# Six pieces of a recurrent scan's side work are put into other steps: the copy of the transposed tokens, a square, the modulation, two shift sums, the last block of x products and the head factors

## The reference

```python
def step(h, xt):                      # h: [8, 128]
    m = concatenate([xt, h], -1) @ weight + bias
    g = sigmoid(m[:, :128] + 1.0); c = tanh(m[:, 128:])
    h_new = g * h + (1.0 - g) * c
    return h_new, h_new
x = x + swapaxes(scan(step, cond, swapaxes(x, 0, 1))[1], 0, 1)
```

```python
ada = t_emb @ w_ada + b_ada           # six sections: sh, sc, g for attention; sh, sc, g for the MLP
xn = layer_norm(logmap0(x));  xm = expmap0(xn * (1 + sc_msa) + sh_msa)
q, k, v = (_to_heads(plin(xm, w, b)) for (w, b) in qkv)       # 16 heads of 8
attn = softmax(q @ k.T / sqrt(8));  out_h = expmap0(attn @ v)
x1 = mobius_add(x, expmap0(g_msa * logmap0(plin(_from_heads(out_h), w_o, b_o))))
xm = expmap0(layer_norm(logmap0(x1)) * (1 + sc_mlp) + sh_mlp)
out = mobius_add(x1, expmap0(g_mlp * logmap0(plin(plin(xm, w_f1, b_f1), w_f2, b_f2))))
x = x + out
```

## Time and profile before

| | us |
|---|---|
| three runs | 461.93, 460.52, 459.68 (median 460.52) |
| the profiled execution, from outside | 461.86 |
| its span | 460.0 |
| busy: DVE, PE, ACT, POOL | 342.5, 346.1, 275.7, 78.9 |
| first state of the scan, last state | 15.33, 294.03 |

### The profile page before, as it was taken

The page is one execution under the profiler, slowest core; times in us unless marked ns, Lnnn a source line. Parts: engine busy times, 40 slices in busy tenths (PEclk is TensorE's granted clock), DMA queues, the critical chain, the costliest instruction groups (busy, mean ns, idle before and its releaser), DMA issues.

```text
span 460.0 us, 11582 instructions
## 1 busy us (share of the span) xinstructions
PE 346.1 (75%) x3768; PEld 217.2 (47%) x3768; DVE 342.5 (74%) x1943; ACT 275.7 (60%) x1030; POOL 78.9 (17%) x152
## 2 busy tenths in 40 slices
PE   1887798797747786747897988989589889767932
PEld 1644565455535454535554645536344446446510
DVE  5578766786899887899887888744933388699883
ACT  2344654446557546557667566636688888954852
POOL 7000000021000021000022000032200115265580
PEclk9999999999999999999999999976679989996877
DMA  7201920010000000000000000000000000000102
GB/s 183 59 2 30 211 40 2 1 35 15 1 1 3 0 2 1 1 1 2 1 2 3 0 1 2 2 3 3 1 2 3 1 3 3 2 1 1 25 0 68
DMA packets 9118, 8.28 MB, mean 18 GB/s; under 512 B 1282, under 2 KB 7700, under 8 KB 9060
## 3 DMA queue, kind: packets, MB, share of 16 engines
q1 hardware_dynamic: 8964, 7.29, 6.9%
q0 software_dynamic: 96, 0.26, 0.2%
HBM read 6.47 MB, written 1.08 MB: 16 GB/s over the span
## 4 chain that ended last, share of the span: by engine, by line
DVE 45%; PE 31%; ACT 12%; issue 7%; POOL 2%; DMA 1%; SPq 0%; DVEq 0%; ACTq 0%; POOLq 0%
DVE guessed L1630 8%; DVE state L1630 8%; PE zb L847 5%; DVE sets L1651 5%; DVE rest L1649 5%; ACT sets L1323 4%; PE tb L974 3%; PE firsts L1145 3%; PE tb L785 3%; ACT prd L1487 2%; PE zb L1125 2%; PE zb L824 2%; PE firsts L1030 2%; ACT prd L1467 1%; PE tb L945 1%
## 5 line engine op out<-in xcount | busy, mean ns | idle before, releaser
L1323 ACT ACTIVATE sets<-zb 128x32 f32<-128x32 f32 x479 | 106.2, 227 | 110.5 <-PE zb L847 101.3
L847 PE MATMUL zb<-guessed,whh 128*128 128x8 f16 x960 | 64.7, 173 | 23.7 <-DVE guessed L1630 1.0
L1630 DVE TENSOR_TENSOR_SCAN state<-sets 128x32 f32<-128x32 f32 x256 | 57.0, 223 | 34.1 <-ACT sets L1323 32.5
L847 PE MATMUL zb<-rest,whh 128*128 128x8 f16 x480 | 51.8, 178 | 32.7 <-DVE rest L1649 31.6
L847 PEld LDWEIGHTS zb<-rest,whh 128*128 128x128 f16 x480 | 35.8, 113 | 80.1 <-DVE rest L1649 74.7
L1630 DVE TENSOR_TENSOR_SCAN guessed<-sets 128x32 f16<-128x32 f32 x255 | 57.4, 225 | 10.9 <-ACT sets L1323 2.9
L847 PEld LDWEIGHTS zb<-guessed,whh 128*128 128x128 f16 x960 | 44.5, 108 | 42.0 <-DVE guessed L1630 36.9
L1649 DVE TENSOR_TENSOR rest<-state,guessed 128x8 f16<-128x8 f32 x255 | 42.6, 167 | 8.7
L1487 ACT ACTIVATE prd<-zb 128x640 f32<-128x640 f32 x64 | 41.9, 711 | 5.7 <-PE zb L1125 5.0
L1651 DVE COPY sets<-state 128x32 f32<-128x32 f32 x255 | 45.0, 176 | 0.0
L641 POOL TENSOR_TENSOR stat<-mv 128x4 f32<-128x4 f32 x4 | 0.8, 202 | 219.5 <-DVE mv L1761 219.5
(11 more groups left out here) (370 smaller groups left out, 693.1 us busy)
## 6 DMA issues: line engine op xcount, KB each, us to landing
mod<-ada_rows SPq DMA_DIRECT2D x4, 768.0 KB, 11.0
resid<-in_x_dram SPq DMA_DIRECT2D x6, 128.0 KB, 3.6
ffz<-shift_rows SPq DMA_DIRECT2D x4, 131.0 KB, 3.2
out_dram<-state SPq DMA_DIRECT2D x8, 64.0 KB, 2.1
out_dram<-early SPq DMA_DIRECT2D x8, 64.0 KB, 2.1
yy<-in_L_cond_w_ada_dram SPq DMA_DIRECT2D x1, 384.0 KB
early<-in_L_cond_weight_dram SPq DMA_DIRECT2D x2, 128.0 KB
resid<-in_x_dram POOLq DMA_DIRECT2D x2, 128.0 KB, 3.5
```

The source lines that it names most:

```text
L847: return pe.matmul(bank[:, 256 * k + i:256 * k + i + NB], whh[:, half, k, :], h, start=False, stop=False, skip_group_check=True)
L1323: return act.activation(view(sets[:, n, 3:4], [39, 2], [38, 2], [4, NB]), view(bank[:, i:i + 1], [256, 2], [0, 2], [1, NB]), ACT.Tanh, sca ...
L1630: return dve.tensor_tensor_scan(dst, *scan_terms(n), 0.0, ALU.mult, ALU.add)
```

## The change

Six pieces are put elsewhere; none is added or taken away, and each computes what it did.

- `uevac` goes from 29 to 28: ACT copies the transposed tokens a tick earlier, in the slot that had the square of tile 1. That square goes behind it, into the slot of tick 29.
- `modulate` goes from 23 to 22: DVE's four instructions each stand a tick earlier. What they wait for (`tok_xn`) isn't moved.
- PE gets a `yield` behind the last shift product, so that `x_part(2)` begins at tick 77 instead of 76, and all its twelve pieces stand a tick later.
- DVE's two shift sums go from tick 79, where both stood, to ticks 84 and 85.
- In the scan's chunks the first of the two head factor instructions goes into the half step ahead of the guess, the second stays.

```diff
--- before.py
+++ after.py
@@ -74,8 +74,8 @@
 
 
 TOK = dict(
-    transpose=1, resid=5, moments=7, norm=10, artanh=12, rho=19, xn=21, modulate=23, utrans=26,
-    uevac=29, usq=(25, 27), clip=29, qkv=(29, 30, 31, 32, 33, 34, 35, 36), yevac=(31, 33, 35,
+    transpose=1, resid=5, moments=7, norm=10, artanh=12, rho=19, xn=21, modulate=22, utrans=26,
+    uevac=28, usq=(25, 27), clip=29, qkv=(29, 30, 31, 32, 33, 34, 35, 36), yevac=(31, 33, 35,
     37), qsq=(32, 34, 36, 38), qreduce=(34, 36, 38, 40), factor=42, scale=(50, 51, 56, 57),
     high=(51, 52, 57, 59), low=(52, 54, 58, 60), stack=(54, 56, 60, 62), queries=(56, 60, 62,
     64), keys=(58, 61, 63, 65), values=(62, 63, 64, 65, 66, 67, 68, 68), xna=21,
@@ -924,6 +924,7 @@
                 yield
                 pe.matmul(ob[:, 0:NB], gw[:, 0:D], shT[:, :], start=True, stop=True)\
                     .then_inc(shift_ps, 1)
+                yield
                 for c in range(2, NC):
                     yield from at_ticks(now, CH * (c - 1) + 8)
                     yield from x_part(c)
@@ -1401,13 +1402,15 @@
                     yield from at_ticks(now, base + T["usq"][1])
                     act.wait_ge(tok_u, c + 1)
                     squares_of((0,))
-                    if c < NC - 1:
-                        yield
-                    squares_of((1,)).then_inc(tok_usq, 1)
+                    if c == NC - 1:
+                        squares_of((1,)).then_inc(tok_usq, 1)
                     yield from at_ticks(now, base + T["uevac"])
                     act.wait_ge(tok_uT_ps, c + 1)
                     act.activation(tuT[:, :, :], tb[:, 1, :].rearrange("p (j t) -> p j t", j=NJ),
                                    ACT.Copy).then_inc(tok_uT, 1)
+                    if c < NC - 1:
+                        yield
+                        squares_of((1,)).then_inc(tok_usq, 1)
                     for j in range(NJ):
                         n = NJ * c + j
                         yield from at_ticks(now, base + T["qsq"][j])
@@ -1676,11 +1679,12 @@
                     if q < 3:
                         yield from whole(now)
                 i.then_inc(ada_sb, 1)
-                yield from at_ticks(now, 79)
+                yield from at_ticks(now, 84)
                 dve.wait_ge(shift_sb, 1)
                 sh = ada[:, 3 * D:4 * D]
                 dve.tensor_tensor_reduce(shift_junk[:, 0, :], sh, sh, 1.0, 0.0, ALU.mult, ALU.add,
                                          shift[:, D:D + 1])
+                yield from whole(now)
                 dve.tensor_tensor_reduce(shift_junk[:, 1, :], sh, shG[:, :], 1.0, 0.0, ALU.mult, ALU.add,
                                          shift[:, D + 1:D + 2]).then_inc(shift_rows, 1)
                 yield
@@ -1900,10 +1904,16 @@
                     i = dve.scalar_tensor_tensor(r, t, 1.5, r, ALU.add, ALU.mult)
                 done_(i)
                 mark = done[0]
-                yield from at_ticks(now, base + T["hfac"])
+                yield from at_ticks(now, base + T["hfac"] - (0.5 if in_scan else 0))
                 settle(mark)
-                settled(dve.tensor_scalar(ht[:, NH4:NA4], hy[:, NH4:NA4], C_HEAD * M_CLIP, C_HEAD, ALU.mult,
-                                          ALU.min))
+                done_(dve.tensor_scalar(ht[:, NH4:NA4], hy[:, NH4:NA4], C_HEAD * M_CLIP, C_HEAD, ALU.mult,
+                                        ALU.min))
+                if in_scan:
+                    mark = done[0]
+                    yield
+                    settle(mark)
+                else:
+                    settle()
                 dve.scalar_tensor_tensor(hfac[:, :, :].rearrange("p q (a h) -> p (q a) h", h=NH),
                                          hy[:, 0:NH4].rearrange("p (a h) -> p a h", h=NH), M_CLIP,
                                          view(ht[:, NH4:NH4 + 1], [1, 12], [0, NH]), ALU.mult, ALU.min)\
```

## The result

| | before | after |
|---|---|---|
| median of four runs, us | 460.6 (459.68 to 461.93) | 456.51 (455.78 to 456.81) |
| ratio, 95% interval | | 0.9896 (0.9879 to 0.9913) |
| profiled execution from outside, its span | 461.86, 460.0 | 455.78, 453.8 |
| states 0 to 255 (the scan) | 278.70 | 274.30 |
| last state to the end (the tail) | 165.97 | 164.19 |

The change takes 4.1 us off (460.6 - 456.51), 1.04%, where 456.7 had been forecast and 3.87 worked out. The two profiled executions first shown lie 6.1 us apart. The second profiles, told with the experiments, say how to split that: the scan is 278.31 - 274.18 = 4.13 us shorter, and the rest is a tail that changes from one execution to the next.

A forecast was written before the change was run, and what follows sets the result against it. The scan was taken as bound by tick length, the recurrence going round DVE, PE and ACT. Gains and costs summed to 3.87 us off the 460.52 median: 456.7 us forecast, range 455.0 to 459.6.

The forecast's parts named there:

- x products: PE, tick 76: x products begun a tick after the last shift product gain 0.40 us, bounds 0.1 and 0.5.
- The copy earlier: Tick 29 of each chunk: PE no longer waits for ACT's copy, 2.26 to 1.29 us, 0.97 a chunk, 2.91 in all.
- the first rival: Projection pieces ahead of `rest`: without the stall's lead three more cost 0.3 each per chunk, 2.7 us back, 459.3; chance 0.09.
- the upper bound: Tick 29: first projection piece also takes only 0.99 us, so 1.27 a chunk, 3.8 us in all.
- The copy's cost in tick 28: ACT, tick 28: copy ends 0.12 us past the next tanh's place; 0.10 a chunk, -0.30, bounds 0 and -0.36.
- The bound at 0: ACT, tick 28: the favourable end of the range, in which the copy costs its new tick nothing.
- The clip factor's margin: Tick 31: POOL's factor, later with the moved square, is still ready 0.3 us before DVE needs it; costs nothing.
- What the modulation gives: PE's second pair of transposes no longer waits for DVE's modulation: 0.16 us a chunk, 0.48, bounds 0 and 0.51.
- What it costs: DVE waits for ACT's normalizations, 0.05 us twice a chunk, plus a store in the third chunk: -0.35, bounds 0 and -0.8.
- Shift sums: DVE, tick 79: 0.36 us gained less 0.08 in ticks 84 and 85, +0.28, bounds 0.1 and 0.36.
- Head factors: DVE: splitting the dependent pair takes the tick from 1.15 to 0.99 us, 0.15 a chunk, +0.45, bounds 0 and 0.45.
- The rival of the tail's clock: Tail after the scan: two more slices at the low clock lose 8 us, 464.7 us; slower had chance 0.04.

## Why the prediction was right, step by step

The mechanism was the one given: three projections that waited for a copy in the same tick number. The sum was 3.87, the scan gave 4.13. Nearly all of the miss is the copy's cost in its new tick, 0.30. That the rest adds up so well has some luck in it: the x products and shift sums were taken 0.12 too low and the head factors 0.12 too high.

1. *The copy earlier*: right. 0.97 a chunk had been worked out; ticks 93, 157 and 221 fell by 0.95 to 0.97. Tick 94 stayed at 1.00, so PE's lead came from a tick of 1.28 as well as from the one of 2.26. With it the first rival falls, in which all eight pieces cost, and the upper bound (no cost of the first piece) too.
2. *The copy's cost in tick 28*: the term that was mis-sized. -0.30 had been taken, 0 was measured: ticks 92, 156 and 220 are 0.99 to 1.00 with the copy in them. The forecast had the copy end 0.12 behind the place of the tanh. The copy started 0.24 after the state instead of the 0.27 taken, and the tanh started 0.09 before the copy's end. The bound at 0 held, the middle didn't. The rest is right in kind: put 0.3 us of square there too and the tick is late. The clip factor's margin is 0.6; the forecast had 0.3, and by its own terms (2.96 less 0.86 and 1.69) it should have been 0.4. What is left of the difference is that the square is 0.30 long and not the 0.59 that the forecast gave it.
3. *What the modulation gives*: right, 0.16, 0.17 and 0.15 in ticks 91, 155 and 219, 0.48 forecast.
4. *What it costs*: 0.35 forecast, 0.30 measured, as 0.48 less the 0.18 left in the table. Nearly as much as it gives, and the kernel without it is as fast.
5. *x products*: 0.40 forecast. Tick 76 fell from 1.49 to 1.04, and the tick at the end of the twelve pieces didn't grow by more than 0.02: about 0.45, nearer the bound of 0.5. The forecast had added 0.10 of cost that isn't there.
6. *Shift sums*: 0.28 forecast, tick 79 fell from 1.35 to 1.03, 0.32, and nothing to be seen in 84 and 85.
7. *Head factors*: right in two chunks (0.15 each), wrong in the third (0.03 instead of 0.15). The forecast carried the first chunk's tick over to the third without looking at it. In the third an extra 0.14 lies before the second factor instruction: it starts 0.84 after the state, where it had started 0.88 after it before, and the store and the next state follow it at about the same distances as before. The rule of the Trainium skill, "VectorE: DVE Perf Modes", section "The DRAIN you can't avoid", taken as the forecast took it, would have made this edit worth nothing. The same section adds that a next instruction that isn't held starts earlier, and with that the trace agrees: 0.55 from state to guess with the instruction between them and 0.55 without. Where the section says that a semaphore costs nothing extra, the trace differs: in the kernel before, of the two factor instructions in one tick the second, which waits for the first, starts 0.19 behind it, while the instructions of the changed kernel without such a wait start 0.08 and 0.09 apart (`rest`, copies of h, first factor instruction). Here the measurement decides.

The rival of the tail's clock didn't come about: no slice more at the low clock, and the last state's 4.1 us arrive at the end. What was not foreseen is that the tail moves by 2.4 us between executions that run the same code. That the point where the level changes varies from run to run, as the Trainium skill says in "TensorE: Matmul & The Clock Gate", section "What's actually happening", agrees with the short windows above, 1.00 and 0.50 at the same distance from the last state. It makes a comparison of two single spans good to 2 us only, while the scans compare to 0.4.

One figure of the forecast's opening is off and bears on nothing else: 278.7 less 255 ticks of 0.99 leaves 26 us lost to side work, not 25.

What stays open: the 0.14 us before the factor instruction of the third chunk, and whether the clock alone sets the tail's length within its 2.4 us.

## What to carry to other kernels

Where a producer and its consumer have the same step number on two engines, read which engine reaches its slot first. Here the consumer did: it sat idle for 0.78 us behind a copy of 0.59, the tick lost 0.96, and one step apart took all of that away. Side work on two engines costs less in the same tick than in neighbouring ones, if each alone would make the tick long (1.27 with projection and evacuation together, 1.29 and 1.20 apart): so keep such pieces together when one of them is moved. Price a moved piece in the tick to which it goes, and in every repetition of the pattern: the third chunk had another neighbour. Judge such edits by the distance of the recurrence's own instructions rather than by the whole time, since an unrelated stage can vary by more than half of what the edit brings.

## What the runs showed of the hardware that was not expected

- ACT starts its next instruction before the reported end of the one ahead (changed kernel, then copy and square in tick 28): copy at 110.35 for 0.59, tanh at 110.85, 0.09 early. With a square next it is the same (copy to 111.09, square at 110.97).
- Behind a late tick a projection piece of 0.99 us costs next to nothing (tick 93 of the run with copy and square in tick 28: 1.04), behind a plain one it costs 0.28 (tick 93 of the changed kernel); it starts 0.30 or 0.03 ahead of the state. That holds where DVE has no piece of its own: with its evacuation of 0.59 us the tick takes 1.20 all the same.
- The tail at the same code: 164.2 to 166.6 us, PE busy from 122.8 to 126.5 in it, and the clock's first fall 11.2 to 14.3 us after the last state.
